# Expert rows of eight tiles summed on TensorE in place of four, with new instruction sequences for the end of the program

## The reference

```
x = x + 0.5 * ffn(layernorm(x))
x = x + attn(layernorm(x))      # 16 heads of 128
x = x + 0.5 * ffn(layernorm(x))
```

```
logits = flat @ router_w.T                 # 64 experts, the best 4 of each token
y = (silu(xg @ gate) * (xg @ up)) @ down   # on at most 32 tokens of each expert
out[token] += y * weight                   # four expert rows for each token
out += (silu(flat @ sh_gate) * (flat @ sh_up)) @ sh_down   # shared part
```

## Time and profile before

| what | value |
|---|---|
| median of 3 runs | 976.5 us (974.59 to 977.72) |
| the profiled execution | 972.94 us, span 971.2 us |
| TensorE busy | 915.0 us, 94% |
| VectorE busy | 763.6 us, 79% |
| ScalarE busy | 646.6 us, 67% |
| GpSimd busy | 645.6 us, 66% |
| mean granted TensorE clock | 0.988 |

### The profile page before, as it was taken

How to read it: one execution, slowest core, us unless ns; L and a number is a source line. 1 busy time by engine, 2 the same in 40 slices (tenths; PEclk the granted TensorE clock), 3 DMA queues, 4 the chain that set the end, 5 groups by cost and what they waited for, 6 DMA issues and landing times.

```text
span 971.2 us, 18502 instructions
## 1 busy us (share of the span) xinstructions
PE 915.0 (94%) x5770; PEld 561.1 (58%) x5772; DVE 763.6 (79%) x2079; ACT 646.6 (67%) x1426; POOL 645.6 (66%) x607
## 2 busy tenths in 40 slices
PE   4999789999999999999999999999999999978987
PEld 3766466555555555555555555555555555765666
DVE  6954399998888888888888888888878789876247
ACT  5634446877778687777778778777777787543431
POOL 3368778878676868778676766867677455236741
PEclk9999989999999999999999999999999999988999
DMA  8979745666765868797785766756575564485757
GB/s 338 356 247 316 270 163 163 100 136 109 153 129 101 169 151 185 141 223 158 177 192 98 153 104 137 153 103 140 107 151 96 90 120 87 89 334 153 250 204 273
DMA packets 302978, 165.58 MB, mean 170 GB/s; under 512 B 278176, under 2 KB 285600, under 8 KB 300832
## 3 DMA queue, kind: packets, MB, share of 16 engines
q1 hardware_dynamic: 297696, 146.56, 62.7%
q0 software_dynamic: 3072, 9.44, 3.0%
q10 hardware_dynamic: 2112, 8.39, 2.1%
HBM read 68.93 MB, written 28.31 MB: 100 GB/s over the span
## 4 chain that ended last, share of the span: by engine, by line
PE 75%; DVE 13%; DMA 4%; issue 3%; ACT 2%; SPq 1%; another core or an unknown queue 0%; POOL 0%; DVEq 0%; ACTq 0%
PE b_p L110 5%; PE b_o L110 5%; PE b_o L111 5%; PE b_o L112 5%; PE b_p L111 5%; PE b_p L112 5%; PE b_s L110 5%; PE b_s L112 5%; PE b_s L111 5%; PE b_out L110 3%; PE b_out L112 3%; PE b_out L111 3%; PE b_v L110 2%; PE b_v L112 2%; PE b_v L111 2%
## 5 line engine op out<-in xcount | busy, mean ns | idle before, releaser
L2452 POOL TENSOR_TENSOR h<-pr,h 128x512 f16<-128x512 f32 x256 | 293.1, 1158 | 160.6 <-ACT h L1171 155.1
L1161 ACT ACTIVATE pr<-b_s,nmax,kappa 128x512 f32<-128x512 f32 x256 | 197.5, 774 | 41.1 <-DVE nmax L1907 36.7
L1904 DVE TENSOR_SCALAR_CACHE_REDUCE junk<-b_s 128x512 bf16<-128x512 f32 x256 | 175.3, 685 | 22.6 <-PE b_s L112 17.5
L1171 ACT ACTIVATE h<-pr 128x512 f16<-128x512 f32 x256 | 153.3, 626 | 0.7 <-DMA pT<-h 0.4
L1935 DVE SCALAR_TENSOR_TENSOR x<-b_out,rinv,x 128x256 f32<-128x256 f32 x256 | 111.4, 476 | 41.8 <-PE b_out L112 40.3
L110 PE MATMUL b_p<-xh,w 128*128 128x512 f16 x256 | 97.8, 382 | 3.1 <-DVE qT L1846 2.2
L110 PE MATMUL b_o<-pT,v 128*128 128x512 f16 x256 | 97.1, 379 | 1.7 <-DVE oT L1923 1.7
L111 PE MATMUL b_p<-xh,w 128*128 128x512 f16 x256 | 97.8, 382 | 0.0
L110 PE MATMUL b_s<-kT,qT 128*128 128x512 f16 x256 | 97.1, 379 | 0.7 <-ACT pr L1161 0.7
L112 PE MATMUL b_p<-xh,w 128*128 128x512 f16 x256 | 97.6, 381 | 0.0
L111 PE MATMUL b_s<-kT,qT 128*128 128x512 f16 x256 | 97.1, 379 | 0.0
(11 more groups left out here) (223 smaller groups left out, 2234.1 us busy)
## 6 DMA issues: line engine op xcount, KB each, us to landing
raw<-in_experts SPq DMA_DIRECT2D x32, 768.0 KB, 8.0
raw_cs<-in_heads SPq DMA_DIRECT2D x16, 1024.0 KB, 5.2
zrows<-zero ACTq DMA_DIRECT2D x4, 2048.0 KB, 11.5
z<-zrows SPq DMA_DIRECT2D x16, 512.0 KB, 4.2
zrows<-zero SPq DMA_DIRECT2D x16, 512.0 KB, 3.9
zl<-zrows SPq DMA_DIRECT2D x16, 512.0 KB, 8.8
rows<-xn SPq DMA_DIRECT2D x8, 512.0 KB, 10.7
pT<-h SPq DMA_TRANSPOSE x256, 3.2
```

What stands on the lines that cost most here:

```text
L1161: act.activation(pr[n % 4][:], b_s[n % 3][:], ACT.Exp, bias=nmax[:, u % 2, i:i + 1], scale=kappa[:, s:s + 1], accum_out=rsum[:, u % 2, i:i ...
L1171: act.activation(h[n % 4][:, 0, :], pr[n % 4][:], ACT.Copy).then_inc(q["p_high"], 1)
L1904: dve.tensor_scalar(junk[n % 2][:], b_s[n % 3][:], 0.0, None, ALU.add, ALU.max, accum_out=peaks[:, n % 2:n % 2 + 1]).then_inc(q["peak_read ...
L2452: pool.tensor_tensor(h[n % 4][:, 1, :], pr[n % 4][:], h[n % 4][:, 0, :], ALU.subtract).then_inc(q["p_split"], 1)
```

## The change

TensorE sums the expert rows of tiles 8 to 15 (two chunks, c = 6 and 7) in place of 12 to 15. `expert_sums` and the special case in `down` give way to `down_with_rows(c)`: all 48 matmuls of the `down` first, piece by piece, then 16 matmuls with `twice` for the chunk's four tiles, with a signal after each two tiles. `combine(24)` to `combine(27)` are gone from VectorE. `store_x(8)` to `store_x(11)` wait for the shared add alone. The order of calls is new on all five engines from the 57th unit to the end; `gate_up(27)` stands after the last expert, and `gate_up(29)` before the `down` of chunk 6.

```diff
-            def expert_sums(c):
+            def down_with_rows(c):
+                pe.wait_ge(q["x_added"], 2 * c)
+                for mi in range(SM):
+                    pe.wait_ge(q["hlo_done"], SM * c + mi + 1)
+                    for t in range(4):
+                        mm3(pe, tb[t // 2][:, (t % 2) * D:(t % 2 + 1) * D], [u[:, mi, t * P:(t + 1) * P] for u in hT],
+                            [u[:, mi, :] for u in dw], mi == 0 and t % 2 == 0, False)
                 pe.wait_ge(q["consts"], CONSTS + 3)
                 for t in range(4):
-                    pe.wait_ge(zl_in[4 * (c - NCH) + t], 32)
+                    i = 4 * (c - NCH) + t
+                    pe.wait_ge(zl_in[i], 32)
                     for k in range(K):
-                        pe.matmul(tb[t // 2][:, (t % 2) * D:(t % 2 + 1) * D], twice[:], zl[4 * (c - NCH) + t][:, k * D:(k + 1) * D],
-                                  start=False, stop=False)
+                        ins = pe.matmul(tb[t // 2][:, (t % 2) * D:(t % 2 + 1) * D], twice[:], zl[i][:, k * D:(k + 1) * D],
+                                        start=False, stop=(t % 2 == 1 and k == K - 1))
+                    if t % 2 == 1:
+                        ins.then_inc(q["down_done"], 1)
...
             expert_out(28)
             expert_hidden(29)
-            gate_up(27)
             expert_hidden(30)
...
             expert_out(31)
+            gate_up(27)
             gate_up(28)
-            down(6)
             gate_up(29)
+            down_with_rows(6)
             gate_up(30)
             gate_up(31)
-            down(7)
+            down_with_rows(7)
...
             combine(21)
             combine(22)
             combine(23)
-            combine(24)
-            combine(25)
             hidden(30)
             hidden(31)
-            combine(26)
-            combine(27)
             add_shared(7)
...
             def store_x(i):
-                if i < 12:
+                if i < SUMMED:
                     sp.wait_ge(q["x_done"], 8 + i + 1)
                     sp.wait_ge(q["x_added"], 2 * (NCH + i // 4 + 1))
                 else:
-                    sp.wait_ge(q["x_added"], 2 * (NCH + 3) + (i - 12) // 2 + 1)
+                    sp.wait_ge(q["x_added"], 2 * NCH + i // 2 + 1)
...
             probs_values(56, 2)
+            probs_values(56, 3)
             output(55, 1)
-            probs_values(56, 3)
```

More of the change, by code:

```diff
@@ L46 @@
 PBITS = 15
+SUMMED = 8
 BIASED = 2
@@ L403, in down @@
                     pe.wait_ge(q["x_added"], 2 * c)
[L404 to L412, removed]
+                for t in range(4):
+                    for mi in range(SM):
+                        ins = mm3(pe, tb[t // 2][:, (t % 2) * D:(t % 2 + 1) * D], [u[:, mi, t * P:(t + 1) * P] for u in hT],
+                                  [u[:, mi, :] for u in dw], mi == 0, mi == SM - 1)
+                    if t % 2 == 1:
                         ins.then_inc(q["down_done"], 1)
@@ L1521, in _ @@
             outputs(59)
+            keys_of(63)
             exps(61, 3)
@@ L1619, in _ @@
             expert_out(24)
+            gathered(27)
             expert_hidden(25)
@@ L1637, in _ @@
             expert_out(27)
+            expert_hidden(28)
+            hidden_high(26)
             expert_out(28)
@@ L1647, in _ @@
             expert_hidden(31)
+            expert_out(31)
             silu(27)
-            expert_out(31)
+            silu(28)
             hidden_high(27)
-            silu(28)
             silu(29)
@@ L2162, in _ @@
             values(57)
+            add(54, 0)
             maxima(56, 3)
-            add(54, 0)
             maxima(57, 0)
             maxima(57, 1)
+            queries(58)
             keys_of(58)
-            queries(58)
             maxima(57, 2)
@@ L2175, in _ @@
             maxima(58, 0)
+            add(55, 0)
             queries(59)
-            add(55, 0)
             values(59)
@@ L2187, in _ @@
             maxima(59, 0)
+            keys_of(60)
             sums(57)
@@ L2190, in _ @@
             maxima(59, 1)
-            keys_of(60)
             maxima(59, 2)
-            maxima(59, 3)
             add(56, 0)
             outputs(57)
+            maxima(59, 3)
             keys_of(61)
             maxima(60, 0)
+            sums(59)
             add(56, 1)
@@ L2202, in _ @@
             maxima(60, 2)
-            sums(59)
+            values(60)
             maxima(60, 3)
-            values(60)
             maxima(61, 0)
@@ L2297, in _ @@
             slot_weights(24)
+            expert_hidden(22)
             slot_weights(25)
@@ L2707, in _ @@
             probs_low(62, 2)
+            power(9)
             probs_low(62, 3)
@@ L2739, in _ @@
             gather(27)
+            scatter(16)
             gather(28)
-            scatter(16)
             scatter(17)
@@ L3018, in _ @@
             load(18)
+            store_rows(8)
+            store_rows(9)
             load(19)
-            store_rows(9)
+            load(20)
             store_rows(10)
-            load(20)
             store_rows(11)
```

76 lines of the change are left out of this document (33 added, 43 removed).

## The result

The changed kernel takes 987.5 us (median of 4 runs, 984.76 to 989.56), the kernel before 975.6 us (4 runs, 973.39 to 977.72): a ratio of 1.0117, interval 1.0090 to 1.0145, or 11.9 us more. The profiled execution took 986.79 us with a span of 985.1, against 972.94 and 971.2: 13.9 us more. The profile before lies 2.6 us under its median and the profile after 0.7 under its own, so the two differences are 1.9 us apart. The prediction was 990.0 us, +13.5. All times and ratios are of fast executions; one execution of the kernel before, 1106.92 us at a mean clock of 0.836, is left out of the last group of the experiments.

The account below looks back on a forecast made before the run. The prediction took TensorE, busy for 94% of the span, as the fuller engine. Its terms, 11.1 us at full clock, +2.9 for the clock and -0.5 for the sequences, gave 13.5 on 976.5: 990.0 us, range 981.5 to 994.

Parts of the forecast that it names:

- The last expert and the scatter: End of the experts: without `gate_up(27)` ahead, TensorE finishes 1.7 us earlier, last scatter and `zl` loads 1.3 us earlier.
- gate_up 27 to 29: TensorE after the experts: three in a row, each waiting for the previous `hid`, starting 930.0, 934.4, 938.9, ending 941.7.
- The new wait for `zl[8]`: TensorE's sums of tiles 8 to 11 wait for that load until 948.7, then take 7.15 us, to 955.85.
- What is late next: VectorE: `add_shared(6)` and four combines delay `hid` 30 and 31 to 964.6; TensorE waits 3.0 us in the last `down`.
- The tail: From TensorE's last end to the span's end: 4.9 us instead of 5.2, one store pair fewer queued.
- The clock: Last `down`: the 3.0 us wait brings TensorE to half speed for 6.8 us, costing +2.9 us.
- The sequences from unit 57 on: Same instructions in another order at the attention's end: a gain of 0.5 us, bounds -1.0 and +1.0.
- (a): Rival at the end: pieces are late but the clock does not fall, 987.1 us; chance 0.25.
- (b): Rival at the end: VectorE's order does no harm, only TensorE's added work counts, +8.1 less 0.5, 984.1 us; chance 0.15.
- (c): Rival, stretch 850 to 890: new sequences close its idle time and clock loss, so not slower, about 976; chance 0.08.
- (d): Rival, 933 to 949: three gaps cause a second clock fall, 2 to 4 us more, about 993; chance 0.10.

Follow-up runs that it names:

- Experiment 11: Changed kernel with combines 20 to 23 ahead of `add_shared(6)` on VectorE instead of behind it: ratio to the kernel before 1.0049, tail 48.72 us.
- experiment 4: Kernel before, four tiles, with only its sums moved behind all four pieces of the last `down`: ratio to the kernel before 1.0058, tail +6.2 us.
- experiment 5: Changed kernel with the sums of tiles 8 to 11 given back to VectorE, new order kept: ratio to the kernel before 1.0078, tail 49.62 us.
- 7: Changed kernel run again unaltered, on the second group's chip: ratio to the kernel before 1.0103, tail 54.23 us.
- 1: Changed kernel with `hidden(30)` and `hidden(31)` placed between combines 20 to 23 on VectorE: ratio to the kernel before 1.0070, tail 49.72 us.
- 2: Changed kernel with the sums of tiles 12 to 15 between second and third piece of the last `down`: ratio to the kernel before 1.0076, tail 49.40 us.
- experiment 3: Changed kernel with ten unused matmuls before the last `down`'s third quarter, filling TensorE's wait: ratio to the kernel before 1.0115, tail 52.18 us.
- experiment 9: Eight tiles summed on TensorE, two pairs of banks in turn, calls reordered to remove waits: ratio to the kernel before 1.0024, tail 46.16 us.
- 10: Kernel before, four tiles, with two pairs of banks in turn for `gate_up(27)` to `(31)` and earlier `hidden` calls: ratio 0.9974, tail 40.19 us.

## Why the prediction was right, and where it was off

- **The last expert and the scatter** (TensorE through 1.7 us earlier, last scatter 1.3 us earlier): 929.43 against 931.06 is 1.63, and the last scatter is at 931.23, 1.28 earlier. Right. It landed in 2.39 us and not 3.17, so the first `zl` load was issued about 2 us earlier.
- **gate_up 27 to 29** (starts 930.0, 934.4, 938.9): 934.57 and 939.00. Right.
- **The new wait for `zl[8]`** (sums from 948.7 to 955.85): 949.08 to 956.24. The load was issued 1.4 us earlier, at 938.89, and took 0.35 us longer.
- **What is late next** (combines to 964.6, `hid` at 964.6, TensorE waiting 3.0 us): `hid` at 964.90, the wait 3.10. The overlap with GpSimd was sized at 1.9 us. Two rows of 0.42 took 1.40 each, 1.96 more; the forecast had 1.9. The two VectorE rows end at 958.98 and 960.41, beside GpSimd's two rows from 957.31 to 960.13. By the exclusion that the Trainium skill states (SBUF — State Buffer, section "Who interferes with whom") the prediction allowed up to 2.5; the trace agrees with an exclusion, at 1.96 us. Experiment 11 confirms the order as the cause.
- **The tail** (4.9 us from TensorE's end to the span's): 985.1 - 980.22 = 4.9.
- **The clock** (+2.9): 24 matmuls lost 2.7 us in one execution and 1.7 in another. It fell in all four profiles whose last `down` waits 3.0 us or more (after, 4, 5, 7), and in none of the four that fill or remove the wait (1, 2, 3, 11). But the prediction's ground was weaker than it took it to be. The wait of 2.26 us ahead of 882.91 stands in all 13 profiles (2.26 or 2.27 us); the clock went to the lower level in its last 0.6 us in 6 (before, 1, 4, 5, 7, 9) and stayed at 1.00 for 5 us or more in 7, the profile after among them. Nor does the longest gap decide: in experiment 5 the clock fell at 955.1 after gaps of 1.28 and 0.94 us, each shorter than the 1.74 that left it up, in a stretch where TensorE was busy 6.6 of 10 us (946 to 956). The lag and the length, taken as fixed at 1.8 and 6.8 us, were 2.0 and 6.8 in one profile of the changed kernel, 3.9 and 3.4 in the other. So the mechanism was right, and that 2.9 met 2.7 was in part luck.
- **The sequences from unit 57 on** (-0.5): a gain of some 0.5 us is there at 823 and gone by 898.68. The error was to carry it to the end of the span without a look at what stands between; the term should have been zero.
- **The sum:** 13.5 against 13.9 on the profile and 11.9 by the medians. Of the 2.5 us between 990.0 and 987.5, 0.9 is the median before, 976.5 by three runs and 975.6 by four, and 1.6 is the difference itself. The four executions of the changed kernel had spans of 983.1 to 987.8 and mean clocks of 0.992 to 0.984, the two longer ones with the lower clocks. The 1.6 us lie inside that spread; the term on the clock, which differs by 1 us from one profile to another, can be a part of it, which no run settles.

On the rivals: (a), no fall of the clock, did not come in either profile of the changed kernel, but after the 2.26 us of the earlier trace rows the clock fell in only 6 of 13 profiles, so it was a fair rival. That every execution has the fall is not shown. (b), TensorE's work alone, does not hold for the changed kernel, whose wait is 3.1 us, but experiments 1 and 2 are kernels like it, +7.9 and +7.6 where (b) had 8.1 at full clock. (c) did not come, and the profile shows how far it was off: half of the clock's loss in 850 to 890 is absent there, and the matmuls at 898.68 start no earlier for it, since TensorE waits for gathered tokens instead. (d) did not come: the gaps of 1.5, 1.4 and 1.4 us left the clock up.

What the prediction had in the sum but did not say is how the parts share it. With 12.5 to 13.9 in all, by tails: the late `hid` without cover, with the clock, 4.6 to 6 us (experiments 1 and 2). Then 7.6 to 7.9 are left. They agree with the account of the first profile, 13.85 less 3.10 of wait and 2.7 of clock, 8.05. The kernel without these waits has +4.4, so about 3 us are left for the gaps before `gate_up` 28 and 29 and before the first sums, 4.3 us in the profile after (a difference of two kernels that also differ in the place of the sums; no run takes these gaps away alone). The +4.4 are 7.15 us of matmuls less the waits that the kernel before has and experiment 9 does not. And a part that I had not looked at by itself: putting the sums last costs 6 us even with four tiles (experiment 4), since it uncovers a wait that the kernel before has too, 3.8 us in that trace and some 5.7 had TensorE come in time.

## What to carry to other kernels

Moving work from an engine with slack to the fuller one costs about its own length there (6 of 7.15 us, experiments 9 and 10), once the waits are gone; before moving it, look whether both are equally full in the stretch that ends last. Work without an open dependency is a cover: find the wait behind it in the trace of before, and don't move it past that wait. When an instruction of an in-order engine waits on something that the change has made later, look at what stands behind it and is ready: four ready combines behind one add cost 4.5 to 6 us here, once no work covered the wait, nearly as much as the matmuls that the change added. And a gain far from the end counts only if the trace shows nothing between that waits for something else: 0.5 us of new order, and a stretch at full clock in place of the lower one, were both gone by 898.68.

## What the runs showed of the hardware

- The same wait does not always bring the clock down: after the 2.26 us ahead of the token choice's last step it fell in 6 of 13 profiles. The low clock after the same wait of about 3 us lasted 6.8 us in one execution and 3.4 us in another of the same kernel. In experiment 5 it began inside the wait of 6.35 us and still held at its end. In the changed kernel's end gaps of 1.36 to 1.50 us left it at 1.00, and in experiment 3 one of 0.69; in experiment 5's expert part it fell after gaps of 1.28 and 0.94.
- VectorE's rows with two inputs in SBUF stretch when they meet a GpSimd row on SBUF: 0.42 to 1.40 us twice, 0.68 to 1.78 once (938.87), beside GpSimd rows on SBUF (one of 1.28 us at 938.82, two in 2.82 us at 957.31).
- The same program took 975 us in the first measurement and 1001 to 1004 in three later ones, each on a chip of its own. The changed kernel's first score matmul of the attention comes at 151.2 us after the start in its first profile and at 166.4 in the other, so 15 of the 22.6 us between these two spans lie ahead of it; the tails behind the last expert are 55.67 and 54.23. The cause stays open.
